# Two 16-head attentions: scores from strips of 32 rows in high and low parts, and one product of constants per tile

## The reference, cut to what matters

```python
# pairs 2 and 3 (L2, L3); b=2, 512 queries, 77 keys, H=16, DH=8
qh, kh, vh = (proj(q, Wq, bq), proj(k, Wk, bk), proj(v, Wv, bv))   # proj: x @ W + bias, split in heads
scores = jnp.einsum('bhqd,bhkd->bhqk', qh, kh) / math.sqrt(DH)
scores = jnp.where(mask, -jnp.inf, scores)                          # L2 only
attn = jax.nn.softmax(scores, axis=-1)
out = jnp.einsum('bhqk,bhkd->bhqd', attn, vh).reshape(b, -1, D) @ Wo + bo
x = x + out
```

## Time and profile before

| | |
|---|---|
| device time, median of 3 runs | 549.51 us (549.36 to 553.01) |
| the profiled execution | 553.62 us, span from first to last instruction 551.9 us |
| PE busy | 476.9 us, 86% of the span |
| DVE, ACT, POOL busy | 347.1, 253.0, 138.9 us |
| chain of work that ended last | 70% PE, 17% DVE |
| the loop over 8 tiles of layer 0 and of layer 1 | about 318 to 374 us and 422 to 478 us of the span |
| mean granted clock of TensorE | 0.911 |

### The profile page before, as it was taken

How to read it: one execution, slowest core, us unless ns; L and a number is a source line. 1 busy time by engine, 2 the same in 40 slices (tenths; PEclk the granted TensorE clock), 3 DMA queues, 4 the chain that set the end, 5 groups by cost and what they waited for, 6 DMA issues and landing times.

```text
span 551.9 us, 8050 instructions
## 1 busy us (share of the span) xinstructions
PE 476.9 (86%) x2704; PEld 380.4 (69%) x2705; DVE 347.1 (63%) x777; ACT 253.0 (46%) x470; POOL 138.9 (25%) x208
## 2 busy tenths in 40 slices
PE   8679999999999998999999879998628999968085
PEld 4558988999999984889978558885224698733034
DVE  3647787777777758423376766616677664176984
ACT  3547766776777662434312224521440544105811
POOL 4240032321300003102036346514623543010000
PEclk9979999999999999979986899979759998989579
DMA  5779000000000000000000000000000000000001
GB/s 174 236 157 69 3 1 2 0 0 0 0 0 0 1 0 1 0 2 1 0 1 0 1 1 1 0 2 1 0 1 0 1 1 0 1 1 0 0 0 39
DMA packets 28157, 9.63 MB, mean 17 GB/s; under 512 B 17855, under 2 KB 26849, under 8 KB 28129
## 3 DMA queue, kind: packets, MB, share of 16 engines
q1 hardware_dynamic: 26876, 8.66, 8.3%
q10 hardware_dynamic: 1253, 0.61, 0.4%
HBM read 8.74 MB, written 0.52 MB: 17 GB/s over the span
## 4 chain that ended last, share of the span: by engine, by line
PE 70%; DVE 17%; ACT 4%; issue 3%; POOL 2%; DMA 2%; SPq 1%; POOLq 0%; DVEq 0%; ACTq 0%
PE bank L1048 6%; PE bank L463 6%; PE bank L458 6%; PE bank L1083 5%; PE bank L825 5%; PE bank L465 5%; PE bank L464 5%; PE bank L963 5%; PE bank L815 4%; PE bank L814 4%; PE bank L1062 3%; PE bank L846 2%; PE bank L1212 2%; DVE stats L1524 2%; DMA shared<-in_L_xattn_Wo 2%
## 5 line engine op out<-in xcount | busy, mean ns | idle before, releaser
L1596 DVE TENSOR_TENSOR probT_lo<-bank,probT_hi 128x512 fp32r<-128x512 f32 (+1 forms) x80 | 55.1, 689 | 25.1 <-ACT probT_hi L1297 24.5
L458 PE MATMUL bank<-ones 128*128 128x512 f32 x118 | 67.9, 715 | 1.8 <-POOL ident L533 1.8
L1297 ACT ACTIVATE probT_hi<-bank 128x512 fp32r<-128x512 f32 (+1 forms) x80 | 47.6, 594 | 41.2 <-PE bank L825 41.1
L1589 DVE TENSOR_REDUCE neg_max<-bank 128x1 f32<-128x589 f32 x64 | 49.1, 768 | 18.9 <-PE bank L815 17.5
L1288 ACT ACTIVATE shared<-bank,neg_max 128x589 f32<-128x589 f32 x64 | 48.0, 750 | 5.9 <-DVE neg_max L1589 5.8
L602 POOL TENSOR_TENSOR rstd<-var_eps,minus_half 128x4 f32<-128x4 f32 x14 | 14.8, 1058 | 135.5 <-DVE var_eps L1530 135.5
L825 PE MATMUL bank<-ident,shared 128*128 128x128 f32 (+1 forms) x320 | 48.0, 272 | 0.4 <-ACT shared L1288 0.4
L678 POOL TENSOR_TENSOR scratch<-scratch,neg_max 128x1232 f32<-128x1232 f32 x16 | 36.0, 2248 | 40.3 <-DVE neg_max L1866 40.3
L458 PEld LDWEIGHTS bank<-ones 128*128 128x128 f32 x118 | 25.8, 235 | 25.9 <-issue 24.0
L825 PEld LDWEIGHTS bank<-ident,shared 128*128 128x128 f32 (+1 forms) x320 | 39.8, 142 | 2.8 <-ACT shared L1288 0.6
L1048 PE MATMUL bank<-k_blocks,queries 128*128 128x308 f32 x128 | 36.3, 427 | 5.9 <-DVE scratch L1840 2.2
(11 more groups left out here) (341 smaller groups left out, 1135.9 us busy)
## 6 DMA issues: line engine op xcount, KB each, us to landing
shared<-in_mask_Bx16xSxS_bk SPq DMA_DIRECT2D x8, 154.0 KB, 8.2
shared<-in_L_xattn_Wkv SPq DMA_DIRECT2D x4, 256.0 KB, 7.1
w<-in_L_ffn_W SPq DMA_DIRECT2D x1, 1024.0 KB
shared<-in_L_xattn_Wq SPq DMA_DIRECT2D x2, 256.0 KB, 5.6
x_residual<-in_x ACTq DMA_DIRECT2D x2, 256.0 KB, 6.3
shared<-in_L_xattn_Wo SPq DMA_DIRECT2D x2, 256.0 KB, 8.6
out_x<-x_residual SPq DMA_DIRECT2D x1, 512.0 KB, 3.2
bo<-in_L_xattn_bo SPq DMA_DIRECT2D x3, 64.0 KB, 3.2
```

Of the source, the lines that this page charges most:

```text
L458: nc.tensor.matmul(bank[:, at, :].rearrange("p (n m) -> p n m", n=4), ones[:], ones[:].unsqueeze(1).to_broadcast([P, 4, P]), start=True, s ...
L1297: nc.scalar.activation(probT[HI][0:n, SLOT[c], :], bank[0:n, PT_BANK[b][c], :], ACT.Copy)\
L1589: nc.vector.tensor_reduce(neg_max[:, b, i:i + 1], scores0(i), AX.X, ALU.max, negate=True)\
L1596: nc.vector.tensor_tensor(probT[LO][0:n, SLOT[c], :], bank[0:n, PT_BANK[b][c], :], probT[HI][0:n, SLOT[c], :].bitcast(F32), ALU.subtract). ...
```

## The change

The scores of a tile now come from four strips of 32 contracted rows (4 heads each) instead of 128 rows filled mostly with zeros. Strip g of the queries is multiplied with `k_blocks[...][32 g : 32 (g+1)]`, 4 heads x 77 = 308 columns, into bank g. Queries and keys are kept in high and low parts of type fp32r, so that a tile takes 3 x 4 products of one instruction each. The scale 1/sqrt(8) moves from the queries to the keys (`bk16` instead of `bq16`). The low part of the queries is a new DVE instruction per batch, ahead of the loop; the high part is the ACT instruction that was there. The queries of both batches are made before the first scores. POOL builds a quarter as many key columns (`k_quad`), rounds them and subtracts. From t = 1 to t = 6 PE runs one 128x256 product of constants between averages and transposes.

```diff
+        k_quad = sb("k_quad", [P, 4, NC])
+        k_blocks = [sb(f"k_blocks_{n}", [P, B, 4, NC], F32R) for n in ("hi", "lo")]
@@ keep_warm: the number of 128-column blocks is now a parameter (n=4)
+        def keep_warm(at, count, n=4):
@@ POOL, spread_kv
-                    nc.gpsimd.tensor_tensor(k_blocks[:, b], k16T[:, n, b, :].unsqueeze(1).to_broadcast([P, HM, NC]),
-                                            head_of_row[:].unsqueeze(2).to_broadcast([P, HM, NC]), ALU.mult)\
+                    own.add(nc.gpsimd.tensor_tensor(k_quad[:], k16T[:, n, b, :].unsqueeze(1).to_broadcast([P, 4, NC]),
+                                                    quad_of_row[:].unsqueeze(2).to_broadcast([P, 4, NC]), ALU.mult))
+                    own.settle()
+                    own.add(nc.gpsimd.tensor_copy(k_blocks[HI][:, b], k_quad[:]))
+                    own.settle()
+                    own.add(nc.gpsimd.tensor_tensor(k_blocks[LO][:, b], k_quad[:], k_blocks[HI][:, b].bitcast(F32),
+                                                    ALU.subtract))
+                    own.settle()
@@ PE, scores
-                    for g in range(4):
-                        last = nc.tensor.matmul(bank[:, g, 0:BK * NC], q,
-                                                k_blocks[:, b, BK * g:BK * (g + 1), :].rearrange("p h k -> p (h k)"),
-                                                start=True, stop=True)
+                    for stationary, moving in ((HI, HI), (HI, LO), (LO, HI)):
+                        begin, end = stationary == moving, stationary == LO
+                        for g in range(4):
+                            rows = slice(32 * g, 32 * (g + 1))
+                            last = nc.tensor.matmul(bank[:, g, 0:BK * NC],
+                                                    qT[stationary][rows, b, (t % TPB) * P:(t % TPB + 1) * P],
+                                                    k_blocks[moving][rows, b].rearrange("p h k -> p (h k)"),
+                                                    start=begin, stop=end)
@@ PE, attention16
                 queries_of(0)
                 keep_warm(4, 1)
-                pe.wait_ge(kv16_spread, 8 * B * (n + 1))
+                queries_of(1)
+                pe.wait_ge(kv16_spread, 7 * B * (n + 1))
                 scores(0)
                 scores(1)
-                queries_of(1)
                 for t in range(NT + 1):
...
                     if t:
                         averages(t - 1)
+                        if t < NT - 1:
+                            keep_warm(4, 1, 2)
                     if t < NT:
                         transposes(t)
@@ ACT, attention16
-                    nc.scalar.activation(q16T[:, b, :], bank[:, 6 + b, :], ACT.Identity, bias=bq16[:, n:n + 1],
-                                         scale=SC16).then_inc(q16_ok, 1)
+                    nc.scalar.activation(qT[HI][:, b, :], bank[:, 6 + b, :], ACT.Identity,
+                                         bias=vec_cols[:, row_q:row_q + 1]).then_inc(q16_hi_ok, 1)
@@ DVE, attention16, ahead of the loop
+                for b in range(B):
+                    dve.wait_ge(q16_hi_ok, B * n + b + 1)
+                    nc.vector.scalar_tensor_tensor(out=qT[LO][:, b, :], in0=bank[:, 6 + b, :],
+                                                   scalar=vec_cols[:, row_q:row_q + 1],
+                                                   in1=qT[HI][:, b, :].bitcast(F32), op0=ALU.add, op1=ALU.subtract)\
+                        .then_inc(q16_ok, 1)
```

More of the change, by code:

```diff
@@ L194, in build @@
         bo16 = sb("bo16", [P, 2, D])
-        bq16 = sb("bq16", [P, 2])
+        bk16 = sb("bk16", [P, 2])
         head_of_row = sb("head_of_row", [P, HM])
+        quad_pair = sb("quad_pair", [P, 2, 4])
+        quad_of_row = sb("quad_of_row", [P, 4])
         half_of_row = sb("half_of_row", [P, 2])
@@ L201, in build @@
         k16T = sb("k16T", [P, 2, B, NC])
-        k_blocks = sb("k_blocks", [P, B, HM, NC])
+        k_quad = sb("k_quad", [P, 4, NC])
+        k_blocks = [sb(f"k_blocks_{n}", [P, B, 4, NC], F32R) for n in ("hi", "lo")]
         v_pair = sb("v_pair", [P, 2, B, D])
@@ L362, in build @@
         q16_in_psum = sem("q16_in_psum")
+        q16_hi_ok = sem("q16_hi_ok")
         q16_ok = sem("q16_ok")
@@ L453, in from_unit @@
             return not isinstance(u, int) or u >= n
-        def keep_warm(at, count):
+        def keep_warm(at, count, n=4):
             for _ in range(count):
-                nc.tensor.matmul(bank[:, at, :].rearrange("p (n m) -> p n m", n=4), ones[:],
-                                 ones[:].unsqueeze(1).to_broadcast([P, 4, P]), start=True, stop=True)
+                nc.tensor.matmul(bank[:, at, 0:n * P].rearrange("p (n m) -> p n m", n=n), ones[:],
+                                 ones[:].unsqueeze(1).to_broadcast([P, n, P]), start=True, stop=True)
         def split_matmul(out, lhsT, rhs, first=True, last=True):
@@ L587, in _ @@
                 own.settle()
+            own.add(nc.gpsimd.tensor_tensor(quad_pair[:], head_of_row[:, 0:8].rearrange("p (g j) -> p g j", g=2),
+                                            head_of_row[:, 8:16].rearrange("p (g j) -> p g j", g=2), ALU.add))
+            own.settle()
+            own.add(nc.gpsimd.tensor_tensor(quad_of_row[:], quad_pair[:, 0, :], quad_pair[:, 1, :], ALU.add))
+            own.settle()
             pool.wait_ge(cT_ok, 2)
@@ L655, in spread_kv @@
                 for b in range(B):
-                    nc.gpsimd.tensor_tensor(k_blocks[:, b], k16T[:, n, b, :].unsqueeze(1).to_broadcast([P, HM, NC]),
-                                            head_of_row[:].unsqueeze(2).to_broadcast([P, HM, NC]), ALU.mult)\
+                    own.add(nc.gpsimd.tensor_tensor(k_quad[:], k16T[:, n, b, :].unsqueeze(1).to_broadcast([P, 4, NC]),
+                                                    quad_of_row[:].unsqueeze(2).to_broadcast([P, 4, NC]), ALU.mult))
+                    own.settle()
+                    own.add(nc.gpsimd.tensor_copy(k_blocks[HI][:, b], k_quad[:]))
+                    own.settle()
+                    own.add(nc.gpsimd.tensor_tensor(k_blocks[LO][:, b], k_quad[:], k_blocks[HI][:, b].bitcast(F32),
+                                                    ALU.subtract))
+                    own.settle()
+                    nc.gpsimd.tensor_copy(va_pair[:, n, b, :, :, DH], half_of_row[:].unsqueeze(1).to_broadcast([P, NPAIR, 2]))\
                         .then_inc(kv16_spread, 1)
-                    half = half_of_row[:].unsqueeze(1)
                     by_pair = v_pair[:, n, b, :].rearrange("p (c h d) -> p c h d", c=NPAIR, h=2)
@@ L1336, in _ @@
             for n in range(2):
-                row = vrow[f"L{n + 2}_xattn_bq"][0] - FIRST
-                nc.scalar.activation(bq16[:, n:n + 1], bank[:, 1, row:row + 1], ACT.Copy, scale=SC16)\
+                row = vrow[f"L{n + 2}_xattn_bk"][0] - FIRST
+                nc.scalar.activation(bk16[:, n:n + 1], bank[:, 1, row:row + 1], ACT.Copy, scale=SC16)\
                     .then_inc(vcol_ok, 1)
@@ L1381, in keys_values @@
                 act.wait_ge(kv16_in_psum, n + 1)
-                row = vrow[f"L{n + 2}_xattn_bk"][0]
                 nc.scalar.activation(k16T[:, n], bank[:, 0, 0:B * NC].rearrange("p (b k) -> p b k", b=B), ACT.Identity,
-                                     bias=vec_cols[:, row:row + 1]).then_inc(kv16_ok, 1)
+                                     bias=bk16[:, n:n + 1], scale=SC16).then_inc(kv16_ok, 1)
                 nc.scalar.activation(v_pair[:, n], bank[:, 1, 0:B * D].rearrange("p (b d) -> p b d", b=B), ACT.Copy)\
@@ L1391, in attention16 @@
                 norm_copy(k)
+                row_q = vrow[f"L{n + 2}_xattn_bq"][0]
                 for b in range(B):
                     act.wait_ge(q16_in_psum, B * n + b + 1)
-                    nc.scalar.activation(q16T[:, b, :], bank[:, 6 + b, :], ACT.Identity, bias=bq16[:, n:n + 1],
-                                         scale=SC16).then_inc(q16_ok, 1)
+                    nc.scalar.activation(qT[HI][:, b, :], bank[:, 6 + b, :], ACT.Identity,
+                                         bias=vec_cols[:, row_q:row_q + 1]).then_inc(q16_hi_ok, 1)
                 for t in range(NT + 1):
```

3 lines of the change are left out of this document (removed).

## The result

The changed kernel takes 563.32 us (median of 4 runs, 559.72 to 564.12), the kernel before 549.43 us on the same chip (median of 4, 548.68 to 553.01). The ratio is 1.023, with a 95% interval of 1.016 to 1.029: slower by 13.9 us. The forecast was 572 us in a range of 546 to 606.

The account below looks back on a forecast made before the run. PE alone was taken to set the 5.35 us turn. Three more low turns per layer (11.9) less 0.8 from high turns gave +11.1 us, +22 in two layers: 549.5 + 22 = 572 us, range 546 to 606.

Parts of the forecast that it names:

- the ring: High-clock loop turn through evacuation wait, averages, constants, transposes: 5.15 us, or 5.01 with scores, against 5.35; gain 0.2 to 0.35.
- The scores: A tile's twelve strip products on PE: 1.3 us taken, range 0.43 (side by side) to 1.72 (serial), 2.08 before.
- The constants: Two 256-column instructions between averages and transposes: about 0.43 us a turn, from a 512-column query product of 0.87.
- The low turn: A loop turn at granted clock 0.50: 8.6 us with the wait, 10.0 with scores, mean 9.3, 3.95 above 5.35.
- The low clock as the decisive term: Loop turns with few full-row products fall to 0.50: 4 of 8 per layer, +11.1 us per layer, +22 in two.
- The start: Ahead of the loop, first scores about 0.9 us later but 0.8 shorter: 0, with 0.5 us either way.
- POOL and ACT at nothing: POOL's key building in three steps, 1.7 us in all, and ACT's unchanged instruction count: both cost 0.
- That the clock holds: Rival: no loop turn falls, even at t = 6; 4.3 us gained per layer, 541 us; chance 0.16.
- One fall per layer: Rival: turns run at 5.15 us and the clock falls once near each loop's end; 547.5 us; chance 0.13.
- serial strips: Rival: strips run one after another, scores 1.72 us, 6 of 8 turns low at 10.8 us; 604 us; chance 0.10.
- the row at 235.5: Stretch of the trace before, read as the clock falling amid 16 products of 8 rows with PE busy throughout.
- theory A: Follow-up runs' reading that few full-row products make the clock fall, whatever PE's idle time; for 32-row constants 555 to 570 us.

Follow-up runs that it names:

- e1: The changed kernel without its product of constants between averages and transposes in turns 1 to 6; 556.15 us.
- e6: e5 with one 256-column product of constants in the wait instead of two where a turn has scores; 542.09 us.
- e2: The changed kernel with its constants between averages and transposes removed and two 256-column, 128-row products put ahead of the averages, where PE waits for ACT; 542.11 us.
- e8: The changed kernel with a tile's twelve score products ordered strip by strip instead of one of each strip in turn; 559.14 us (one run).
- e4: The kernel before, scores unchanged, with only the 256-column product of constants between averages and transposes added in turns 1 to 6; 552.34 us.
- e7: The changed kernel plus 512-column products of constants behind the scores of tiles 0, 1 and 2 at the loop's start; 560.20 us, ratio 1.014 to before.
- e3: e2 with 32 instead of 128 contracted rows in the constants in the wait, same columns and place; 579.52 us.
- e5: e2 plus 512-column products of constants behind the scores of tiles 0, 1 and 2 at the loop's start; 541.48 us, ratio 0.981 to before.

## Why the prediction was right, and where it was off

**The bound and the ring: right.** A turn at the high clock is 5.19 us, forecast 5.15 from 1.17 + 0.67 + 1.74 + 0.43 + 1.14 with a wait or 5.01 without. Its parts in the chain: averages 0.67 + 1.74, constants 0.53 instead of 0.43, and from there to the next averages 2.25 us by way of ACT's evacuation, forecast 1.14 + 1.17 = 2.31. The gain against 5.35 is 0.16 us per turn. The 1.4 us that the scores lost came out again as the evacuation and the constants, as written. e1 and e6 confirm the ring from the other side: without the constants in it the same sum is 1.17 + 2.41 + 1.14 = 4.72 us, and their high turns take 4.71.

**The scores: mis-sized.** The step "twelve loads at that pace are 1.31 us. As every new product has its own load, I take 1.3 us" failed: the chain of e2 has 0.63 us at the high clock, that of after 1.07 at the low. The reason was the row chosen for it, 18-column products over all rows, whose loads follow each other; products of different strips start within 0.03 us of each other (e8). The measured value lies nearer to the other end of the bounds, 0.43. The Trainium skill, "TensorE: Matmul & The Clock Gate" (Part 3, packing small matmuls), gave an estimated 0.56 us, and the trace, with 0.63, comes near to it. For the time it mattered little: at the high clock the wait takes up whatever the scores do not use, and only a low turn is shorter by it.

**The constants: 0.53 for 0.43 us.** The query product of 512 columns from which they were scaled takes 0.87 us; half of it is 0.43. The two instructions cost 0.10 us more, in after and in e4 alike, and the transposes behind them 0.03 to 0.05 less; a low turn has 1.03 where 0.86 was forecast.

**The low turn: right.** 8.70 us, forecast 8.6 to 10.0 with 9.3 as the mean; the lower end was right, since the scores are short: averages 1.13 + 3.32, constants 1.03, transposes 2.14, scores 1.07.

**The low clock as the decisive term: right as a mechanism, under half the size.** Forecast were 4 low turns per layer and +11.1 us each. Layer 0 went up by 10.2 us (77.1 to 87.4), layer 1 by nothing (73.9 to 73.7). The step that failed is "I take 4 of 8", as one number for both layers. By the starts of the sixteen 18-column averages of successive tiles, layer 0's turns took 8.6, 8.2, 6.1, 5.2, 7.5, 9.0 and 5.0 us, 49.6 in sum, against 39.4 before: two turns low almost throughout, one of 7.5 and one of 6.1 partly, and the one of 9.0 that was low before too (8.0). For layer 0 the number was about right. In layer 1 they took 6.2, 5.2, 5.2, 6.1, 5.2, 7.1 and 5.0, 40.1 against 39.5 before: its falls met transposes more than averages, and the turn that was slow before was shorter (7.1 for 8.3). That this is chance of the execution rather than a property of layer 1 is suggested by e7 and e8, whose turns hold the same products as those of after: there layer 1 took 79.2 and 79.3 us and layer 0 83.2 both times, and the sum is 162.4 where after has 161.0. So the cost over both layers was +10 to +11.4 us in each of three profiled executions, not +22: the turns that became low are about half as many as forecast. Which turn is hit, and what brings the clock back in one turn and not in the next, is told by no view here and stays open.

**From the sum to the median.** The profiled executions differ by 9.4 us (553.62 to 563.01), the medians by 13.9 (549.43 to 563.32). The gap of 4.5 is that the profiled execution of before lay 4.2 us above its median, which the prediction had said, and that of after 0.3 below its own. Both executions were of the kind that is longer outside the layers, by some 4 to 5 us. If the median run of before was of the other kind, as its 549.43 us suggest, about 4 of the 13.9 us are not the change's, and 572 lies so near to 563 in part by luck: the sum had +22 where the layers show +10. No trace of a shorter run of before was kept.

**The start: right for layer 0.** DVE's first take came 7.79 us after the transposes of the normalised rows (314.00 to 321.79), 7.52 before (312.80 to 320.32): 0.27 later, forecast 0 with 0.5 either way, and the low parts take 0.75 us each for 0.69. In layer 1 the first 18-column averages came 1.2 us sooner in the loop than before (17.5 for 18.7 us after the transposes), which was not forecast. POOL and ACT at nothing: right, 138.1 and 253.4 us busy against 138.9 and 253.0.

**The rivals.** That the clock holds, 541 us, was not what this kernel does. When e2 and e5 made it hold in nearly all turns, they took 542.11 and 541.48 us, near that price, but in part by luck: their turn is another one (4.96 us, forecast 5.15), and their profiled executions are of the kind that is shorter outside the layers. The rival's condition, that the new constants and the strips keep the clock up, failed; with full-row constants in the wait instead it holds in nearly all turns, with 32-row ones it does not (e2, e3). One fall per layer (547.5) and serial strips (604) did not occur. The step that made the forecast right was that products of few rows let the clock fall, and it was read from the row at 235.5. That reading was weaker than the prediction says: the busy 0.50 us lie behind the fall, and PE had waited 1.10 us until 234.24, so it is no fall "without any wait" and could not tell rows from waits. e3 could, and there the guess held.

**A version that beats both.** e2 and e5, the strips with full-row constants in the wait, took 542.11 and 541.48 us, against 563.32 for after; e5 is faster than before by 1.3 to 2.7 per cent on its chip, and 8.2 of its 11.9 us lie in the layers. The strips are worth something (turn 4.96 instead of 5.35 us, and in e5 no fall at t = 6) as soon as full-row work that nobody needs stands where PE would wait.

## What to carry to other kernels

Before splitting a full-row product into strips, write down the turn twice, at both granted clocks, and look in the trace for a place where the clock fell while PE ran few rows. Such a place is a reason for a test and no proof: here only e2 against e3, the same columns over other rows, told rows from waits. If the shortened product uncovers a wait, put unneeded full-row products into that wait and not into the rest of the ring: there most of their time is hidden (with 1.06 us of them a turn of e2 is 4.96 us long, with 0.53 a high turn of e6 4.71), and here they turned a loss of 10 us in the two layers into a gain of 8.2 to 9.5. What a gain leaves uncovered, here the evacuation, caps it whatever the clock does.

## What the runs showed that was not expected

- In e3 the clock fell twice with PE busy for 3.00 of the 3.00 us shown ahead of the fall, in a loop whose only work on more than 32 rows is transposes and averages, and then stayed at 0.50 for 40.50 us. This cost more than theory A expected, 579.52 us for 555 to 570.
- Products of different 32-row strips start out of the order in which the kernel issues them: in e8 the fourth strip's first product is the tenth instruction of a tile's scores, and it starts within 0.03 us of the first. The order in which strips are written changed nothing (0.72 for 0.70 us).
- A product of constants costs 0.53 us in the ring where half of a 512-column one would be 0.43 (after, e4), whether strips stand near it or not.
